# A graph network on one core: the table q made in the layer edge stages instead of the node stages, and a longer lead for the gathers

## The reference, cut to what matters

```python
h = x @ W_enc.T + b_enc
for l in range(2):
    m = jnp.concatenate([h[row], h[col]], axis=-1)
    m = jax.nn.relu(m @ msg_W1[l].T + msg_b1[l])
    m = m @ msg_W2[l].T + msg_b2[l]
    agg = jax.ops.segment_sum(m, col, num_segments=h.shape[0])
    upd = jnp.concatenate([h, agg], axis=-1) @ upd_W[l].T + upd_b[l]
    h = _layer_norm(h + upd, ln_g[l], ln_b[l])
return h @ W_out.T + b_out
```

## Time and profile before

| | us |
|---|---|
| median of 3 runs | 3886.1 (3885.23 to 3891.72) |
| the profiled execution | 3925.8 |
| its span | 3924.1 |

### The profile page before, as it was taken

How to read it: one execution, slowest core, us unless ns; L and a number is a source line. 1 busy time by engine, 2 the same in 40 slices (tenths; PEclk the granted TensorE clock), 3 DMA queues, 4 the chain that set the end, 5 groups by cost and what they waited for, 6 DMA issues and landing times. The chain is left out here.

```text
span 3924.1 us, 93325 instructions
## 1 busy us (share of the span) xinstructions
PE 3146.7 (80%) x25312; PEld 2796.9 (71%) x25312; DVE 2686.3 (68%) x8634; ACT 2361.9 (60%) x5642; POOL 1817.9 (46%) x1782
## 2 busy tenths in 40 slices
PE   4966537766556789978999876999969998778998
PEld 3743326554443379978998776999969988768998
DVE  9999747765436688865666544666647665547998
ACT  3789707655432268875665543566646665436999
POOL 0000133556664533334555564655444555665664
PEclk9989968988778999999999997999989999989999
DMA  0046516765438989995665432899956654426987
GB/s 18 2 143 225 165 38 185 196 173 157 131 100 279 337 294 366 358 331 167 192 187 169 138 110 62 297 323 330 315 190 193 191 173 148 122 72 215 295 295 248
DMA packets 460716, 777.83 MB, mean 198 GB/s; under 512 B 113688, under 2 KB 115864, under 8 KB 460392
## 3 DMA queue, kind: packets, MB, share of 16 engines
q1 hardware_dynamic: 355046, 548.85, 42.3%
q10 hardware_dynamic: 67714, 147.73, 11.0%
q0 software_dynamic: 37632, 77.15, 7.8%
HBM read 451.50 MB, written 321.78 MB: 197 GB/s over the span
## 5 line engine op out<-in xcount | busy, mean ns | idle before, releaser
L885 DVE SCALAR_TENSOR_TENSOR edges_acc<-edges_acc,keep,edges_ps_a 128x128 f32 (+1 forms) x2352 | 820.2, 349 | 374.2 <-remote 121.3
L853 POOL DMA_INDIRECT ring<-table_p,esrc x784 | 760.1, 970 | 640.8 <-PE edges_ps_m L1014 329.8
L1013 PE MATMUL edges_ps_m<-ring,ident 128*128 x3136 | 646.6, 288 | 125.5 <-POOLq L843 50.7
L1014 PE MATMUL edges_ps_m<-edges_q_ring,edges_turned 128*128 x3136 | 632.5, 284 | 27.0 <-issue 26.7
L870 DVE TENSOR_TENSOR edges_onehot<-iota,drel 128x512 f32<-128x512 f16 x441 | 303.6, 689 | 443.5 <-DMA table_p<-nodes_p_out 299.4
L1013 PEld LDWEIGHTS edges_ps_m<-ring,ident 128*128 128x128 f32 x3136 | 499.1, 200 | 148.4 <-issue 98.0
L981 ACT ACTIVATE edges_msg<-edges_ps_m 128x512 f32<-128x512 f32 x392 | 231.4, 590 | 614.3 <-PE edges_ps_m L1014 241.9
L1014 PEld LDWEIGHTS edges_ps_m<-edges_q_ring,edges_turned 128*128 128x128 f32 x3136 | 499.4, 200 | 36.0 <-issue 35.6
L1023 PE MATMUL edges_ps_a<-edges_onehot,edges_msg 128*128 128x128 f32 x3136 | 437.4, 284 | 69.6 <-issue 63.1
L853 POOL DMA_INDIRECT ring<-table_h,esrc x344 | 328.2, 954 | 308.3 <-PE edges_ps_a L1038 157.1
L1023 PEld LDWEIGHTS edges_ps_a<-edges_onehot,edges_msg 128*128 128x128 f32 x3136 | 397.9, 199 | 82.8 <-issue 81.6
(11 more groups left out here) (315 smaller groups left out, 6869.5 us busy)
## 6 DMA issues: line engine op xcount, KB each, us to landing
table_z<-nodes_z_t SPq DMA_DIRECT2D x196, 256.0 KB, 5.0
table_p<-nodes_p_out SPq DMA_DIRECT2D x196, 256.0 KB
table_q<-nodes_q_out ACTq DMA_DIRECT2D x196, 256.0 KB
edges_q_ring<-table_q SPq DMA_DIRECT2D x196, 256.0 KB
edges_d_ring<-table_d ACTq DMA_DIRECT2D x98, 512.0 KB
table_t<-edges_acc SPq DMA_DIRECT2D x196, 256.0 KB
nodes_in_a<-table_t SPq DMA_DIRECT2D x196, 256.0 KB
nodes_in_z<-table_z SPq DMA_DIRECT2D x196, 256.0 KB, 4.5
```

Source lines behind the costliest of these rows:

```text
L853: nc.gpsimd.indirect_dma_start(out=ring[:, e % RE * W:e % RE * W + P], out_offset=None, in_=table[:, :], in_offset=bass.IndirectOffsetOnAx ...
L885: nc.vector.scalar_tensor_tensor(out=to, in0=to, scalar=m.keep[:, s:s + 1], in1=ps_a[:, i % AR, where(j):where(j) + F], op0=ALU.mult, op1= ...
L1013: nc.tensor.matmul(to, m.ident[:], rows[j], start=True, stop=False)
L1014: last = nc.tensor.matmul(to, turned[:, i % QR, j * P:(j + 1) * P], slots[j], start=False, stop=True)
```

## The change

q is no longer made in the node stages of layers -1 and 0: its four matmuls, its copy, its store and their waits go. In the edge stage of layer l, ScalarE loads z chunks (`load_z`, 256 KB each, four buffers; SyncE the first ten), TensorE makes q of chunk i+8 in batch i between `segment` and `combine` (`product_q`, four matmuls into two new PSUM banks), and ScalarE copies it out of PSUM (`copy_q`): the first eight chunks straight into `q_ring`, before the first batch; the other 90 into `q_out`, from which ScalarE stores them to `table_q` two batches later. SyncE loads `q_ring` from there as before, after a wait for the store (`kept_q`). So the 98 products fall in the lead-in and in the first 90 of the 196 batches. AHEAD becomes 64, in all three edge stages.

```diff
@@ -39,7 +39,8 @@
...
 PW = -(-NPAIR // 3)
-AHEAD = 24
+AHEAD = 64
+ZR, QO, LEAD = 4, 5, 8
 EPS = 1e-5
...
@@ -782,7 +783,10 @@
...
             d_ring = sb("d_ring", [P, DR, DB * CH], F16)
-            ps_m = pb("ps_m", 512, QR)
+            ps_m, ps_q = pb("ps_m", 512, QR), pb("ps_q", 512, 2)
+            z_in, q_out = sb("z_in", [P, ZR, CH]), sb("q_out", [P, QO, CH])
+            s_z, s_kept_q = [sem(f"s_z{r}") for r in range(ZR)], [sem(f"s_kept_q{r}") for r in range(QO)]
+            s_made_q, s_copied_q = sem("s_made_q"), sem("s_copied_q")
         else:
...
@@ -793,27 +797,43 @@
...
         s_d = [sem(f"s_d{r}") for r in range(DR)]
-        s_out, s_q, s_go, s_q_first = [sem("s_out0"), sem("s_out1")], [sem("s_q0"), sem("s_q1")], sem("s_go"), sem("s_q_first")
+        s_out, s_q, s_go = [sem("s_out0"), sem("s_out1")], [sem("s_q0"), sem("s_q1")], sem("s_go")
         load = lambda eng, at: nc.values_load_multi_w_load_instructions(
...
         third = lambda words, k: (words[k // 3 % 8] >> (k % 3 * 10)) & 1023
+
+        def load_z(eng, c):
+            if c >= ZR:
+                eng.wait_ge(s_made_q, c - ZR + 1)
+            eng.dma_start(z_in[:, c % ZR, :], m.table_z[layer][turn_back(c) * P:(turn_back(c) + 1) * P, :]).then_inc(s_z[c % ZR], 16)
+
+        def kept_q(eng, c):
+            eng.wait_ge(s_kept_q[(c - RC) % QO], 16 * ((c - RC) // QO + 1))
+
+        def copy_q(eng, copy, c):
+            eng.wait_ge(s_made_q, c + 1)
+            if c >= RC + QO:
+                kept_q(eng, c - QO)
+            to = q_ring[:, c * CH:(c + 1) * CH] if c < RC else q_out[:, (c - RC) % QO, :]
+            copy(to, ps_q[:, c % 2, :]).then_inc(s_copied_q, 1)
+
         with nc.Block() as block:
...
                 if not degrees:
-                    for c in range(RC):
-                        sp.dma_start(q_ring[:, c * CH:(c + 1) * CH], chunk(table_q, turn_back(c))).then_inc(s_q[0] if c else s_q_first, 16)
-                    sp.wait_ge(s_q_first, 16)
+                    for c in range(LEAD + 2):
+                        load_z(sp, c)
+                    sp.wait_ge(s_copied_q, 1)
                     sp.sem_inc(s_n, 1)
-                    sp.wait_ge(s_q[0], 16 * (RC - 1))
+                    sp.wait_ge(s_copied_q, RC)
                 sp.sem_inc(s_n, RC if degrees else RC - 1)
...
                     if not degrees and c + RC < NCHUNK:
-                        sp.wait_ge(s_q[c % 2], 16 * (c // 2 + 1) + (16 * (RC - 1) if c % 2 == 0 else 0))
+                        sp.wait_ge(s_q[c % 2], 16 * (c // 2 + 1))
                     sp.sem_inc(s_n, 1)
...
@@ -828,6 +848,7 @@
...
                         if c + RC < NCHUNK:
+                            kept_q(sp, c + RC)
                             sp.dma_start(q_ring[:, at * CH:(at + 1) * CH], chunk(table_q, turn_back(c + RC))).then_inc(s_q[c % 2], 16)
...
@@ -972,9 +993,18 @@
...
                     turn(1)
+                    for c in range(LEAD):
+                        copy_q(act, nc.scalar.copy, c)
                     for i in range(NB):
...
                             turn(i + 2)
+                        if i + LEAD + 2 < NCHUNK:
+                            load_z(act, i + LEAD + 2)
+                        if i + LEAD < NCHUNK:
+                            copy_q(act, nc.scalar.copy, i + LEAD)
+                        if RC <= i + LEAD - 2 < NCHUNK:
+                            act.wait_ge(s_copied_q, i + LEAD - 1)
+                            act.dma_start(chunk(table_q, turn_back(i + LEAD - 2)), q_out[:, (i + LEAD - 2 - RC) % QO, :]).then_inc(s_kept_q[(i + LEAD - 2 - RC) % QO], 16)
                         act.wait_ge(s_pq, i + 1)
...
@@ -1013,6 +1043,15 @@
...
                     last.then_inc(s_pq, 1)
+
+                def product_q(c):
+                    pe.wait_ge(s_z[c % ZR], 16 * (c // ZR + 1))
+                    if c >= 2:
+                        pe.wait_ge(s_copied_q, c - 1)
+                    for j in range(J):
+                        last = nc.tensor.matmul(ps_q[:, c % 2, j * P:(j + 1) * P], z_in[:, c % ZR, j * P:(j + 1) * P],
+                                                m.wproj[:, layer, D:2 * D], start=True, stop=True)
+                    last.then_inc(s_made_q, 1)
 
...
@@ -1065,9 +1104,14 @@
...
                         segment(i - BEHIND)
+                    if i + LEAD < NCHUNK:
+                        product_q(i + LEAD)
                     if i < NB:
...
 
+                if not degrees:
+                    for c in range(LEAD):
+                        product_q(c)
                 for i in range(NB + 2):
...
@@ -1337,23 +1381,12 @@
...
 
-                def evacuate_q(c, b, turn):
-                    act.wait_ge(s_proj, c + 1)
-                    if reused(c, RING):
-                        act.wait_ge(s_store["q"][b], turn * 16)
-                    nc.scalar.copy(q_out[:, b, :], ps_q[:, b % 2, :]).then_inc(s_out_q, 1)
-
-                def store_q(c, b, turn):
-                    act.wait_ge(s_out_q, c + 1)
-                    act.dma_start(chunk(m.table_q[nxt], c), q_out[:, b, :]).then_inc(s_store["q"][b], 16)
                 root_y = root(mv, rstd, s_aggr, s_std, s_norm)
...
                 else:
-                    pipelined(act, [(root_y, 2), (copy_z, 4), (norm_y, 3), (evacuate_q, 5), (store_q, 6)])
-                    for b in range(RING):
-                        act.wait_ge(s_store["q"][b], 16 * slot_uses(RING, b))
+                    pipelined(act, [(root_y, 2), (copy_z, 4), (norm_y, 3)])
 
...
@@ -1397,15 +1430,12 @@
...
                     if reused(c, 2):
-                        pe.wait_ge(s_v if final else s_out_q, c - 1)
-                        if not final:
-                            pe.wait_ge(s_out_p, c - 1)
+                        pe.wait_ge(s_v if final else s_out_p, c - 1)
                     for j in range(J):
...
                         else:
-                            nc.tensor.matmul(part(ps_q, b % 2, j), part(z_t, b, j), m.wproj[:, nxt, D:2 * D], start=True, stop=True)
                             last = nc.tensor.matmul(part(ps_p, b % 2, j), part(z_t, b, j), m.wproj[:, nxt, 0:D], start=True, stop=True)
...
```

12 lines of the change are left out of this document (6 added, 6 removed).

## The result

The changed kernel takes **4022.4 us** (median of four, 4016.7 to 4031.1) beside 3888.0 for the kernel before: a ratio of 1.0347, with 1.0323 to 1.0371 as its 95% interval. It is 3.5% slower. The forecast was 3843, with a range of 3735 to 3960, so it had the wrong sign and the result lies outside the range.

A forecast was written before the change was run, and what follows sets the result against it. Bounds: TensorE in nodes0 and the edge stages' first part, DMA in nodes -1, gathers in the tails. Terms -34 - 74 + 134 + 60 - 94 - 35 = -43 took 3886.1 to 3843 us; range 3735 to 3960.

The forecast's parts named there:

- Node stages: Without q, nodes -1 falls to 3.10 us a chunk (34 us less) and nodes0 to 3.25 (74 less).
- Products: Making q in 90 batches of each layer edge stage takes 3.70 us a batch, TensorE the bound: 134 us more.
- Rival C: Edge stages: the product part is dearer, 4.10 us a batch with z late: +68, 3911 us; chance 0.10.
- Lead with its start: AHEAD of 64: 94 us less in the layer edge stages, 35 less in edges, against longer stage starts.
- the middles and tails: Layer edge stages after the products: a lead of 64 saves 12 us in the middle and 35 in the tail, each.
- the edges stage: A lead of 64 makes the edges stage 35 us shorter, bounds 10 and 90.
- the start of an edge stage: Lead-in products and 64 gathers without a stop lengthen each layer edge stage's start by 30 us, 60 in all.
- rival A: Starts of edges0 and edges1, and tails: gathers in a run hold up handovers, +126, 4012 us; chance 0.22 in some degree.
- Rival B: Handover delays don't exist outside the profiler, so the lead brings its full 88 and 90: 3662 us; chance 0.15 with its half.
- Rival D: Edge stages: the change doesn't open the lead, GpSimd stays near 24 tiles ahead: 3928 us; chance 0.02.
- signs named beforehand: Marks expected in the later profile, such as GpSimd's first stop in edges0; a node stage saving under half its term refutes.
- The tail's 1.57 us a gather: Forecast wrong if tail gathers stay at this pace and the end of GpSimd's work doesn't move.

The follow-up runs named there:

- n1: Node stages of the changed kernel with the edge stages of the kernel before, lead 24, q never made (p read instead): 3851 us, ratio 0.9805.
- b1: The kernel before with only the lead (AHEAD) raised from 24 to 64, no products: 3970 us, ratio 1.0110.
- a1: The changed kernel with the lead (AHEAD) set back from 64 to 24: 4016 us, ratio 1.0227.
- a7: The changed kernel with a 128x512 GpSimd memset after each gather of the layer edge stages, lead 64: 3881 us, ratio 0.9917.
- a9: The changed kernel with a GpSimd memset after each gather, 128x384 in layer edge stages and 128x256 in planning: 3807 us, ratio 0.9780.
- b5: The kernel before with lead 64 and a 128x256 GpSimd memset after each gather of layer edge stages and planning: 3921 us, ratio 1.0011.
- d1: The kernel before with 48 gathers (24 in a row, 12 pairs with waits) and 24 memsets added on GpSimd in stage place: that stage grew 3 us.

## Why the prediction was wrong, point by point

**Node stages** (forecast -108, n1 -77). The direction was right, the sizes not. In nodes -1 I took VectorE to run full at 3.10 us a chunk. The window has VectorE at 85%, DMA at 0.87, and 29.4 chunks in 100 us, 3.40. Nothing is full; the group of the transposes says what TensorE waits for:

```profile
...
L1425 PE MATMUL nodes_ps_t<-ident,nodes_z 128*128 128x128 f32 x120 | 19.7, 286 | 28.3 <-ACT nodes_z L1364 28.3
...
```

28.3 us in 100 for ScalarE's `nodes_z`. The term was a tenth of a microsecond a chunk over the whole stage (10.5 / 98), not 0.35. In nodes0 it was 0.575 instead of 0.75: TensorE 94% and DMA 0.94 at once, and DMA moved 305 GB/s there, less than the 327 of the earlier trace rows.

**Products** (forecast 134, 150 with their share of the start; measured 165). Right: 3.75 us a batch for 3.70, TensorE the bound; it waited 1.4 us for z in the whole product part. Rival C is out. The DMA share of 0.90 at 289 GB/s again speaks against the 435 GB/s cited with the Trainium skill (Perfetto Trace Analysis, Roofline) as a measure of the room left in this part: at that share all 16 engines full would move an estimated 321. The first loads of edges0 in the kernel before did come near the page's figure: a window from 1754 to 1756 us has a DMA share of 1.02 (all 16 busy) and 409 GB/s.

**Lead with its start** (forecast -94, -35, and the rest of the start +44: -85; measured +41 where the lead stands alone, b1). This is the step that failed. From the forecast of -43 to the +106 of the stages, the two starts were missed by 61 us in all, the node stages by 41, the middles and tails by 26, the edges stage by 13 and the product parts by 8. So the term that failed most is the start of an edge stage, put at +30. I had rival A's rows, priced a held start at up to 65 a stage, and took 30 as "the middle" between bounds that had evidence only at one end. It measured +60 and +61 a stage. b1 has +56 in each of its two starts without any product, and a1, with the products and a lead of 24, has +11. The middles and tails gave 33 and 35 instead of 47, since the handover stops stayed there as I had feared. The edges stage gave 17 to 24.

**Rival A** was right in its main mechanism: the start is held up, by more than the +52 from which it decides, and `msg` of the fourth batch came at 100 us where A said 80. That its total came so near (4012 for 4022) is partly luck: beside the stages of the two profiles, its node stages save 41 us too much and its leads (30 in all, for 90) 60 too little, and the 134 us of the result hold 28 that the stages don't show. And it is not the absence of a stop that holds up handovers: a7 and a9 run on as long and lose nothing.

**Rival B** is out: b1's timed runs are 41 us longer than those of the kernel before beside it, so the delays are there without the profiler. But the argument that I had against B was not sound. I took the 39.7 us between the timed runs and the profiled one as a bound on what the profiler adds, and in its other sets the kernel before takes up to 3928 (median) in its timed runs too. **Rival D** is out: the last gather stands 55 us before the barrier, where it stood 24.

Of the signs named beforehand, GpSimd's first stop after 64 gathers and its last gather some 50 us before the end came as forecast. The tail's 1.57 us a gather stayed, which was half of a sign against the forecast (the other half, an unmoved end of GpSimd's work, didn't come). nodes -1 saved 10.5 us, less than half its term: that sign came in full.

## What to carry to other kernels

A deeper prefetch is not free when the engine that issues it disturbs the others: count what the extra run costs in handovers, and look for the rows that show a handover in such a run before putting a price between two bounds. Where gathers from GpSimd follow each other as fast as it can issue them, try a small instruction after each (here 0.43 us) before giving up on the lead. Where two limits come within 10% of each other, as in both node stages here, don't give a chunk the time of the larger: it took 10 to 13% more. And weigh a change that moves work between stages beside its counterpart without it in the kernel that you would keep.

## What the runs showed of the hardware

- While GpSimd's gathers start 1.25 us apart, ScalarE goes on up to 41 us after the TensorE work that it waits for (b1's second batch, the changed kernel's ninth product), and matmuls without a wait between them stand 2 to 3 us apart (b1). With the gathers 1.45 us apart the effect is weaker (a start of 57 us in b5 for 104 in b1); at 1.67, 1.71 and 2.11 us on the mean it was not seen. Whether the increment travels late or is seen late, and what path the engines share, isn't shown. The Trainium skill (DMA: Bandwidth & Descriptors, SWDGE vs HWDGE vs iDMA) says that GpSimd's software writes the descriptors of such transfers to rings in SBUF; no run here looks at those writes.
- The load on the DMA engines doesn't explain it. In the changed kernel, amid the run, they were three quarters idle:

```profile
...
1726.00:1761.00 35.00, 7.14 (x32) 6.67 (x31) 0.00 (x0) 0.58 (x1) 26.40 (x28) 0.55 0.23 60
...
```

- It isn't only work handed on by TensorE. In planning of the kernel before, during its 48 gathers, VectorE waits for its own counter: the copy of L640 ends at 520.06, and L641, which waits for it, starts 6.67 us later.

```profile
...
519.92 0.14 DVE L640 COPY plan_cols<-plan_ps_s 98x1 f32<-98x1 f32 x1
526.72 0.63 DVE L641 TENSOR_SCALAR plan_ended<-plan_step,plan_cols 98x784 f32<-98x784 f32 x1 [6.67 <-remote]
...
```

- Nor is it GpSimd being busy: in a7 and a9 GpSimd, with its memsets, is busy for more of the start than in the changed kernel (33.09 of 37.5 us in a9, 66.60 of 107.5), and in d1 24 memsets back to back (13 us) cost nothing to be seen.
- Planning, which the change doesn't touch, took 95 to 109 us in the profiles where its 48 gathers follow at 1.25 us, and 82 to 83 in the five with a memset between them.
